# Dense products of two batches leave their bank by ScalarE instead of VectorE's fused blend, and all queues get new orders

## The chip, the cores and the metric

The kernel runs on one core of one Trainium2 chip. The time is the device time of one execution in microseconds (us), the median of several runs. A profiled execution shows every instruction. The engines are TensorE (PE: matrix products, and PEld for its weight loads), VectorE (DVE), ScalarE (ACT), GpSimd (POOL) and SyncE (SP), whose queue (SPq) issues all transfers here. Matrix products are written into banks of PSUM; everything else lies in SBUF, and transfers go between SBUF and the chip's memory (HBM).

## The reference

Four stages run over x of 4 batches x 512 tokens x 512 features, each with a layer norm and a residual:

```python
x = x + attn_a(layernorm(x))   # gelu(x @ (w1.T-w2.T product * sparse_mask) + b2)
x = x + ffn(layernorm(x))
x = x + attn_b(layernorm(x))   # one head of 128: softmax(q k^T) v, times Wo
x = x + ffn(layernorm(x))

def ffn(x):                    # weight 512x512, 64 centroids
    dots = softmax(x @ centroids.T / TEMPERATURE)
    hits = dots > THRESHOLD
    query_sel = any(hits, axis=1)              # per token
    cluster_sel = any(hits, axis=0)            # over ALL tokens
    row_sel = cluster_sel[assignments]         # per output feature
    dense = x @ weight.T + bias
    return where(query_sel[:, None] & row_sel[None, :], dense, 0)
```

The row selection of a feed-forward stage needs the softmax of all 2,048 tokens, so no output of stage 4 can be finished before the clusters of its last batch are known.

## The kernel before

The tokens are cut into 16 tiles of 128 (batch b, tile t; n = 4b + t). Every fp32 operand is split into a high and a low part, so one 128x128 by 128x512 product is three matmuls. Five tables, PE_ORDER, ACT_ORDER, DVE_ORDER, POOL_ORDER and SP_ORDER, list by hand every step of every queue; each engine walks its table from front to back, and a step waits on the semaphores of what it needs. An engine whose next step is not ready waits, and all behind it wait too. PE writes into four banks for products (m_bank) and four for transposes (t_bank). Each kind takes them in rotation in the order of PE_ORDER, so a new tile waits until the tile that stood in the same bank four tiles earlier was taken out (`freed_by`).

Steps of stage 4, for batch b and tile t:

- T.x4.b.t: PE transposes x after stage 3; hi.x4 (ACT) and lo.x4 (DVE) split the result.
- cl4.b.h: products with the centroids (a batch at once, or a half); lgev (ACT, L649) copies them out, tc (PE) transposes them, logit, lmax (DVE, L881 to L888), cexp (ACT, L671) and prob (DVE, L895 to L905) do the softmax. prob writes `qsel` (query_sel of the batch's tokens), `rq` = rstd * qsel, and the running maximum `best`.
- After the last batch, best1 (DVE, L910), bestT (PE, L1070), csel (DVE, L915 and L917) and mask (PE, L1086) turn `best` into a bank that holds row_sel for every token. The rest of `out` hangs on it.
- dn4.b.t.c...: the dense products of a tile, in chunks of the 512 inputs (c02 is chunks 0 and 2). The layer norm's mean lies in the weights, its rstd is applied afterwards.
- qb.b.t (ACT, L719): y_tok = qsel * bias. xb.b.t (POOL, L546): y_tok += x_tok. blend4.b.t (DVE, L925): y_tok = bank * rq + y_tok. That frees the bank.
- out.b.t (DVE, L949) copies y_tok over x_tok where the mask bank says so, and store.b.t (SP) writes the tile to HBM.
- The last tile, 3.3, goes in two halves of 256 columns: dn4h, blend4h (L936), outh (L942), storeh.

Stage 2 has the same steps with a 2. There the dense products already leave through ACT: ev2 (L664, y_tok = rstd * bank), bias2 (POOL, L526), and blend2 or x2 on DVE (L829, L842: y_tok * qsel + x_tok, both operands in SBUF). In stage 3, norm.3, bo.b.t (POOL, L540) and x3.b.t (DVE, L872) appear in the rows below. In stage 1, attn.0.0, attn.0.1 and attn.0.2 are four matmuls each (L1019): w1_hi*w2_hi, w1_hi*w2_lo, w1_lo*w2_hi; T.x1 transposes the normed x of batch 0 (norm.1.0.t on ACT), and w2lo (L738) and w1lo (L743) are the low parts of the weights, made on DVE between the statistics of x (stats, L768 and L769).

Of the kernel before, what the change touches and what calls it, by code (L numbers as in the profile page):

```python
# [26 lines left out]

SQUARED = {2, 3, 4}
# [1157 lines left out]
```

## Time and profile before

| | |
|---|---|
| median of 3 runs | 279.13 us (278.44 to 280.58) |
| the profiled execution | 278.25 us, of which the core's span is 276.5 us |
| PE busy | 268.4 us (97% of the span) |
| DVE, ACT, POOL busy | 196.7, 176.8, 158.8 us (71%, 64%, 57%) |
| TensorE's granted clock over the span | 0.997 of 2.4 GHz |
| HBM read, written | 13.76 MB, 4.19 MB |

Times within the span count from its start. A line number is a line of the kernel before. A row of instructions that are alike is merged ("x6"); its duration is then from the first start to the last end. "[0.59 <-PE ...]" behind a row is the time in which the engine sat idle before it and what ended the wait. PE's matmuls overlap in the pipeline: one is shown 0.39 us long, while the next starts 0.23 us later.

### The profile page before, as it was taken

The page shows a single profiled execution, that of the slowest core. Times are in us where ns is not written, and L with a number is a line of the kernel's source. Part 1 is how long each engine was busy: PE and PEld are TensorE (multiplying, and loading weights), DVE is VectorE, ACT ScalarE, POOL GpSimd, SP SyncE. Part 2 cuts the span into 40 slices and gives each one's busy share as a digit, 9 for nine tenths or more (in the row PEclk, how much of TensorE's full clock was granted, in tenths as well). Part 3 has the DMA queues.
Part 4 walks back from the last instruction along what each step waited for, and adds up shares of the span by engine and source line. Part 5 has one row for each costly group of instructions (what it writes and reads, how often), then busy time and mean ns, then how long its engine had stood idle before and what let it go on. Part 6 is the DMA issues. An engine that isn't in the chain of part 4 may idle for free.

```text
span 276.5 us, 4419 instructions
## 1 busy us (share of the span) xinstructions
PE 268.4 (97%) x1392; PEld 224.2 (81%) x1392; DVE 196.7 (71%) x410; ACT 176.8 (64%) x358; POOL 158.8 (57%) x192
## 2 busy tenths in 40 slices
PE   7899999999999999999999999999999999999894
PEld 7787888888888888789988888888888888877673
DVE  3888988505926867775399796788259466867996
ACT  4855886465476785449899887777645576675400
POOL 4693988265495481289897994970730537113910
PEclk9999999999999999999999999999999999999998
DMA  6999064800000000000000000000000000000087
GB/s 230 356 370 344 12 207 177 303 0 0 2 0 0 2 0 2 2 0 0 2 0 0 4 1 0 2 0 0 2 2 0 0 2 1 0 2 0 13 306 288
DMA packets 10246, 18.23 MB, mean 66 GB/s; under 512 B 1200, under 2 KB 1968, under 8 KB 10224
## 3 DMA queue, kind: packets, MB, share of 16 engines
q1 hardware_dynamic: 10224, 17.96, 18.5%
q8 instruction: 11, 0.18, 0.3%
q14 instruction: 11, 0.09, 0.1%
HBM read 13.76 MB, written 4.19 MB: 65 GB/s over the span
## 4 chain that ended last, share of the span: by engine, by line
PE 88%; issue 4%; POOL 2%; DVE 2%; DMA 2%; ACT 1%; SPq 1%; DVEq 0%; POOLq 0%; ACTq 0%
PE m_bank L966 70%; PE t_bank L1059 11%; PE m_bank L1139 5%; DMA x_tok<-in_L_attn_a_x 2%; POOL y_tok L546 1%; PE t_bank L1065 1%; PE m_bank L1019 1%; DVE y_tok L925 1%; DVE x_tok L949 0%; ACT odd_hi L613 0%; POOL rstd L458 0%; SPq L384 0%; DVE y_tok L936 0%; SPq L387 0%; PE m_bank L1086 0%
## 5 line engine op out<-in xcount | busy, mean ns | idle before, releaser
L966 PE MATMUL m_bank<-ffn_hi,even_hi 128*128 128x512 f32 x96 | 39.0, 406 | 0.2 <-DVE y_tok L925 0.2
L966 PE MATMUL m_bank<-ffn_lo,even_hi 128*128 128x512 f32 x96 | 37.7, 392 | 0.0
L966 PE MATMUL m_bank<-ffn_hi,even_lo 128*128 128x512 f32 x96 | 37.4, 390 | 0.0
L546 POOL TENSOR_TENSOR y_tok<-y_tok,x_tok 128x512 f32<-128x512 f32 x16 | 20.4, 1296 | 25.4 <-ACT y_tok L719 25.4
L570 ACT ACTIVATE ones_and_squares<-x_tok,mv 128x512 bf16<-128x512 f32 x44 | 31.5, 717 | 4.1 <-DVE x_tok L872 3.7
L526 POOL TENSOR_TENSOR y_tok<-y_tok,bias_f 128x512 f32<-128x512 f32 x16 | 20.8, 1314 | 16.2 <-ACT y_tok L664 16.2
L454 POOL TENSOR_SCALAR ve<-mv 128x1 f32<-128x1 f32 (+1 forms) x20 | 5.3, 264 | 36.1 <-ACT ones_and_squares L570 35.0
L458 POOL TENSOR_TENSOR rstd<-ve,half 128x1 f32<-128x1 f32 (+1 forms) x31 | 23.9, 771 | 2.6
L775 DVE TENSOR_TENSOR even_lo<-t_bank,even_hi 128x512 fp32r<-128x512 f32 x24 | 16.2, 683 | 12.7 <-ACT even_hi L613 12.5
L775 DVE TENSOR_TENSOR odd_lo<-t_bank,odd_hi 128x512 fp32r<-128x512 f32 x28 | 18.8, 685 | 6.2 <-ACT odd_hi L613 6.0
L966 PE MATMUL m_bank<-odd_hi,wqkv_hi 128*128 128x512 f32 (+1 forms) x60 | 21.5, 358 | 0.0
L966 PEld LDWEIGHTS m_bank<-ffn_lo,even_hi 128*128 128x128 f32 x96 | 18.0, 188 | 3.9
L540 POOL TENSOR_TENSOR x_tok<-x_tok,bo 128x512 f32<-128x512 f32 x16 | 21.0, 1331 | 0.0
L966 PEld LDWEIGHTS m_bank<-ffn_hi,even_hi 128*128 128x128 f32 x96 | 18.1, 188 | 3.6 <-DVE y_tok L925 0.6
L966 PE MATMUL m_bank<-odd_lo,wqkv_hi 128*128 128x512 f32 (+1 forms) x60 | 20.9, 348 | 0.0
L966 PE MATMUL m_bank<-odd_hi,wqkv_lo 128*128 128x512 f32 (+1 forms) x60 | 20.8, 347 | 0.0
L966 PEld LDWEIGHTS m_bank<-ffn_hi,even_lo 128*128 128x128 f32 x96 | 18.1, 189 | 3.1
L966 PE MATMUL m_bank<-attn_hi,odd_hi 128*128 128x512 f32 x48 | 19.5, 405 | 0.0
L581 ACT ACTIVATE xn_odd<-x_tok,ve,rstd 128x512 f32<-128x512 f32 x20 | 16.1, 811 | 4.8 <-POOL ve L461 4.8
L966 PE MATMUL m_bank<-attn_lo,odd_hi 128*128 128x512 f32 x48 | 18.8, 391 | 0.0
L966 PE MATMUL m_bank<-attn_hi,odd_lo 128*128 128x512 f32 x48 | 18.7, 390 | 0.0
L613 ACT ACTIVATE even_hi<-t_bank 128x512 fp32r<-128x512 f32 x24 | 13.8, 595 | 6.8 <-PE t_bank L1059 6.8
(186 smaller groups left out, 775.2 us busy)
## 6 DMA issues: line engine op xcount, KB each, us to landing
out<-x_tok SPq DMA_DIRECT2D x15, 256.0 KB, 2.3
x_tok<-in_L_attn_a_x SPq DMA_DIRECT2D x3, 1024.0 KB, 8.2
xn_odd<-in_L_attn_a_xt SPq DMA_DIRECT2D x2, 1024.0 KB, 6.5
x_tok<-in_L_attn_a_x SPq DMA_DIRECT2D x4, 256.0 KB, 4.2
y_tok<-in_L_attn_a_w SPq DMA_DIRECT2D x4, 256.0 KB, 5.1
w_raw<-in_L_attn_a_w SPq DMA_DIRECT2D x4, 256.0 KB, 5.3
xt_other<-in_L_ffn_weight SPq DMA_DIRECT2D x4, 256.0 KB, 6.8
y_tok<-in_L_attn_a_sparse_mask SPq DMA_DIRECT2D x4, 256.0 KB, 7.3
```

Of the source, the lines that this page charges most:

```text
L454: link(pool.tensor_scalar(ve[:, i:i + k], mv[:, i:i + k, 1], 1.0 / D ** 3, EPS, ALU.mult, ALU.add))
L458: ins = pool.tensor_tensor(rstd[:, i:i + k], ve[:, i:i + k], half[:, 0:k], ALU.pow)
L526: pool.tensor_tensor(y_tok[:, n, :], y_tok[:, n, :], bias_f[:, :], ALU.add).then_inc(done[kind], 1)
L540: pool.tensor_tensor(x_tok[:, n, :], x_tok[:, n, :], bo[:, :], ALU.add).then_inc(done[kind], 1)
L546: pool.tensor_tensor(y_tok[:, n, :], y_tok[:, n, :], x_tok[:, n, :], ALU.add).then_inc(done[kind], 1)
L570: act.activation(squares, x_tok[:, n, :], ACT.Square, bias=sum_of(*key), scale=-float(D), accum_out=mv[:, i, 1:2]).then_inc(done[kind], 1)
L581: act.activation(xn_odd[:, t, :], x_tok[:, n, :], ACT.Identity, bias=nbias[:, i:i + 1], scale=rstd[:, i:i + 1]).then_inc(done[kind], 1)
L613: act.activation(split_of(what, b, t)[0], bank_view(what, bank_of("T", *key)), ACT.Copy).then_inc(done[kind], 1)
L775: dve.tensor_tensor(lo, bank_view(what, bank_of("T", *key)), f32(hi), ALU.subtract).then_inc(done[kind], 1)
L966: ins = pe.matmul(bank, a, w, start=(first and n == 0), stop=(last and n == count - 1))
L1059: ins = pe.transpose(bank[:, c * r:(c + 1) * r], blk, ident[0:r, 0:r])
L1139: ins = pe.matmul(bank[:, tokens], cen_hl[:, c, :], a[:, c, tokens], start=(c + h == 0), stop=(c == KC - 1 and h == 1))
```

## The change

For the tiles of batches 2 and 3 except 3.3 (seven tiles), the three steps qb, xb and blend4 are replaced. ev4 (ACT) reads the bank and writes y_tok = rstd * bank; bias4 (POOL) adds the bias; blend4 (DVE) computes y_tok * qsel + x_tok with both operands in SBUF. The bank is free after ev4. Each engine has as many steps of these kinds as before.

```diff
+EVICTED = {2, 3}
...
+                elif kind == "bias4":
+                    b, t = key
+                    n = b * TPB + t
+                    pool.wait_ge(*done_at("ev4", (b, t)))
+                    pool.tensor_tensor(y_tok[:, n, :], y_tok[:, n, :], bias_f[:, :], ALU.add).then_inc(done[kind], 1)
...
+                elif kind == "ev4":
+                    b, t = key
+                    n = b * TPB + t
+                    i = 3 * NT + n
+                    act.wait_ge(*done_at("dn4", key))
+                    act.wait_ge(*done_at("rstd", (4, b)))
+                    act.wait_ge(*done_at("x2", (b, t)))
+                    act.activation(y_tok[:, n, :], bank_of("dn4", b, t)[:, :], ACT.Identity,
+                                   scale=rstd[:, i:i + 1]).then_inc(done[kind], 1)
...
+                elif kind == "blend4" and key[0] in EVICTED:
+                    b, t = key
+                    n = b * TPB + t
+                    dve.wait_ge(*done_at("bias4", key))
+                    dve.wait_ge(*done_at("prob", (4, b)))
+                    dve.scalar_tensor_tensor(out=y_tok[:, n, :], in0=y_tok[:, n, :], scalar=qsel[:, 1, n:n + 1],
+                                             in1=x_tok[:, n, :], op0=ALU.mult, op1=ALU.add).then_inc(done[kind], 1)
...
+                if kind == "dn4" and key[0] in EVICTED:
+                    return done_at("ev4", key)
...
```

All five tables are new from their first entry to their last: the tiles of every stage come in another order (PE begins its transposes with tile 0.1 instead of 0.0, for instance), and so do the loads and stores. The number of products, transposes, splits and transfers is the same. SP's last four entries were store.3.1, store.2.2 and the two halves of 3.3; now they are store.3.2, the two halves of 3.3, and store.2.1.

One line of PE_ORDER near its end, before and now:

```diff
-dn4.2.3.c3 dn4.3.0.c31 dn4.3.2.c2 bestT.4 dn4.3.1.c0 dn4.2.2.c1 mask.4 dn4.3.1.c1 dn4.3.2.c03 dn4.2.2.c3
...
+dn4.3.0.c2 bestT.4 dn4.2.2.c0 mask.4 dn4.3.1.c2 dn4.2.2.c3 dn4.3.1.c30 dn4.2.1.c3 dn4.2.2.c21 dn4.3.2.c1
```

PE's first steps. The rows are the two groups of four L1019 matmuls behind the first transpose, before the change; even_lo is w1's low part (w1lo), w2t_lo is w2's (w2lo):

```order
L1019 MATMUL m_bank<-w2t_hi,even_hi 128x512 [waits w1hi_done,w2hi_done,consts]
L1059 MATMUL t_bank<-ident,xn_odd 128x128 [waits norm_done]
L1019 MATMUL m_bank<-w2t_lo,even_hi 128x512 [waits w2lo_done]
L1019 MATMUL m_bank<-w2t_hi,even_lo 128x512 [waits w1lo_done]
L1059 MATMUL t_bank<-ident,xn_odd 128x128 [waits norm_done]
```

The same place of PE in the changed kernel:

```order
L1045 MATMUL m_bank<-w2t_hi,even_hi 128x512 [waits w1hi_done,w2hi_done,consts]
L1085 MATMUL t_bank<-ident,xn_odd 128x128 [waits norm_done]
L1045 MATMUL m_bank<-w2t_hi,even_lo 128x512 [waits w1lo_done]
L1045 MATMUL m_bank<-w2t_lo,even_hi 128x512 [waits w2lo_done]
L1085 MATMUL t_bank<-ident,xn_odd 128x128 [waits norm_done]
```

The group that needs w1's low part now comes ahead of the one that needs w2's.

DVE's queue from best1 of stage 4 to the last output tile, before the change (L925 is blend4, L949 and L942 are out and outh, L936 is blend4h):

```order
L910 TENSOR_REDUCE best<-best 128x64 [waits prob_done]
L925 SCALAR_TENSOR_TENSOR y_tok<-m_bank,rq,y_tok 128x512 [waits prob_done,xb_done,dn4_done]
L915 TENSOR_REDUCE csel<-t_bank 64x1 [waits bestT_done]
L917 TENSOR_SCALAR csel<-csel 64x128 [waits chain]
L925 SCALAR_TENSOR_TENSOR y_tok<-m_bank,rq,y_tok 128x512 [waits prob_done,xb_done,dn4_done]
L949 COPY_PREDICATED x_tok<-m_bank,y_tok 128x512 [waits blend4_done,mask_done] x6
...
L936 SCALAR_TENSOR_TENSOR y_tok<-m_bank,rq,y_tok 128x256 [waits prob_done,xb_done,dn4h_done]
L942 COPY_PREDICATED x_tok<-m_bank,y_tok 128x256 [waits blend4h_done,mask_done] x2
```

The same place of DVE in the changed kernel (L941 is the blend4 of the seven tiles, L973 and L966 are out and outh, L960 is blend4h):

```order
L927 TENSOR_REDUCE best<-best 128x64 [waits prob_done]
L941 SCALAR_TENSOR_TENSOR y_tok<-y_tok,qsel,x_tok 128x512 [waits prob_done,bias4_done]
L932 TENSOR_REDUCE csel<-t_bank 64x1 [waits bestT_done]
L934 TENSOR_SCALAR csel<-csel 64x128 [waits chain]
L941 SCALAR_TENSOR_TENSOR y_tok<-y_tok,qsel,x_tok 128x512 [waits prob_done,bias4_done]
L973 COPY_PREDICATED x_tok<-m_bank,y_tok 128x512 [waits blend4_done,mask_done] x4
L941 SCALAR_TENSOR_TENSOR y_tok<-y_tok,qsel,x_tok 128x512 [waits prob_done,bias4_done]
L973 COPY_PREDICATED x_tok<-m_bank,y_tok 128x512 [waits blend4_done,mask_done] x5
L941 SCALAR_TENSOR_TENSOR y_tok<-y_tok,qsel,x_tok 128x512 [waits prob_done,bias4_done] x2
...
L941 SCALAR_TENSOR_TENSOR y_tok<-y_tok,qsel,x_tok 128x512 [waits prob_done,bias4_done]
L966 COPY_PREDICATED x_tok<-m_bank,y_tok 128x256 [waits blend4h_done,mask_done]
L973 COPY_PREDICATED x_tok<-m_bank,y_tok 128x512 [waits blend4_done,mask_done]
```

The blends read no bank any more, one blend that stood ahead of best1 has moved behind it, five blends of full tiles now stand behind the first out where four stood, and the last entry is a full tile.

ACT's last rows in the changed kernel (L657 is lgev, L679 cexp, L689 ev4, L736 qb); before, the L689 rows were eight L719 rows (qb), two ahead of the last cexp and six behind it:

```order
L657 ACTIVATE lg<-m_bank 128x512 [waits tc_done,cl4_done]
L689 ACTIVATE y_tok<-m_bank,rstd 128x512 [waits x2_done,rstd_done,dn4_done]
L679 ACTIVATE ce<-cl,ncmx,rstd 128x64 [waits lmax_done]
L679 ACTIVATE ce<-cl,ncmx,rstd 128x64 x3
L689 ACTIVATE y_tok<-m_bank,rstd 128x512 [waits x2_done,rstd_done,dn4_done] x2
L736 ACTIVATE y_tok<-bias_f,qsel 128x512 [waits x2_done,prob_done]
L689 ACTIVATE y_tok<-m_bank,rstd 128x512 [waits x2_done,rstd_done,dn4_done] x4
```

ACT's last steps now wait for PE's tiles, where they waited for prob only.

## Rows read from the trace of the kernel before

**Rows 1.** Busy time by stretch: stretch, us, each engine's busy us, clock, DMA share, GB/s.

```profile
220.00:240.00 20.00, 20.00 (x107) 16.80 (x106) 14.19 (x32) 12.23 (x27) 9.73 (x9) 1.00 0.01 1
...
250.00:260.00 10.00, 8.68 (x38) 6.46 (x37) 7.83 (x15) 6.17 (x12) 6.31 (x6) 1.00 0.00 1
```

**Rows 2.** Chain of work that ended last: start us, us, what.

```profile
7.84 0.67 DVE w2t_lo L738
...
70.96 0.44 PE t_bank L1065 x4
71.40 5.49 PE m_bank L966 x24
```

**Rows 3.** Timeline of PE: start, us, line, what, idle before it.

```profile
7.25 0.60 PE L1059 MATMUL t_bank<-ident,xn_odd 128*128 128x128 f32 x4
8.55 1.21 PE L1019 MATMUL m_bank<-w2t_lo,even_hi 128*128 128x512 f32 x4 [0.70 <-DVE w2t_lo L738]
...
10.53 0.60 PE L1059 MATMUL t_bank<-ident,xn_odd 128*128 128x128 f32 x4
...
241.31 0.39 PE L1139 MATMUL m_bank<-even_hi,cen_hl 128*128 128x512 f32 x1
...
249.02 0.63 PE L1065 MATMUL t_bank<-ident,lg 128*128 128x128 f32 x4
...
256.14 0.50 PE L966 MATMUL m_bank<-ffn_hi,odd_hi 128*128 128x512 f32 x1 [0.33 <-DVE y_tok L925]
...
259.60 0.50 PE L1086 MATMUL m_bank<-onehot,csel 128*128 128x512 f32 x1 [0.98 <-DVE y_tok L925]
```

**Rows 4.** Timeline of ACT at the start.

```profile
7.65 0.63 ACT L558 ACTIVATE even_hi<-y_tok 128x512 fp32r<-128x512 f32 x1 [0.68 <-DMA y_tok<-in_L_attn_a_w]
```

**Rows 5.** Timeline of DVE, from the last softmax to the mask.

```profile
253.26 1.30 DVE L897 TENSOR_SCALAR qsel<-crec 128x4 f32<-128x4 f32 x1
...
255.01 0.42 DVE L905 TENSOR_TENSOR best<-best,cl 128x256 f32<-128x256 f32 x1
...
257.58 1.30 DVE L917 TENSOR_SCALAR csel<-csel 64x128 fp32r<-64x128 f32 x1
258.81 0.73 DVE L925 SCALAR_TENSOR_TENSOR y_tok<-m_bank,rq,y_tok 128x512 f32<-128x512 f32 x1
```

**Rows 6.** Timeline of POOL in the same stretch.

```profile
253.26 1.28 POOL L546 TENSOR_TENSOR y_tok<-y_tok,x_tok 128x512 f32<-128x512 f32 x1 [0.95 <-ACT y_tok L719]
256.26 7.54 POOL L546 TENSOR_TENSOR y_tok<-y_tok,x_tok 128x512 f32<-128x512 f32 x6 [1.72 <-ACT y_tok L719]
```

**Rows 7.** Single lines: duration ns min/median/max, first and last start us.

```profile
L897 DVE TENSOR_SCALAR qsel<-crec x8: 169/170/1300, 86.7 to 253.3; 128x4 f32<-128x4 f32 x8
...
L842 DVE SCALAR_TENSOR_TENSOR x_tok<-y_tok,qsel,x_tok x12: 735/752/1436, 122.7 to 174.0; 128x512 f32<-128x512 f32 x12
...
L526 POOL TENSOR_TENSOR y_tok<-y_tok,bias_f x16: 1287/1312/1349, 66.2 to 162.7; 128x512 f32<-128x512 f32 x16
...
L664 ACT ACTIVATE y_tok<-m_bank,rstd x16: 671/687/696, 53.6 to 129.6; 128x512 f32<-128x512 f32 x16
```

**Rows 8.** Timeline of DVE, then of POOL, where stage 2's blend met a POOL operation.

```profile
155.14 1.44 DVE L842 SCALAR_TENSOR_TENSOR x_tok<-y_tok,qsel,x_tok 128x512 f32<-128x512 f32 x1
...
154.74 3.02 POOL L540 TENSOR_TENSOR x_tok<-x_tok,bo 128x512 f32<-128x512 f32 x2
```

**Rows 9.** Timeline of DVE behind the mask: its first and its last row.

```profile
260.13 3.91 DVE L949 COPY_PREDICATED x_tok<-m_bank,y_tok 128x512 f32<-128x512 int32 x6 [0.59 <-PE m_bank L1086]
...
273.42 0.76 DVE L942 COPY_PREDICATED x_tok<-m_bank,y_tok 128x256 f32<-128x256 int32 x2
```

**Rows 10.** Busy time of DVE behind the mask: stretch, us, busy us, clock, DMA.

```profile
260.13:274.20 14.07, 13.77 (x23) 1.00 0.71 266
```

**Rows 11.** Transfers by line: KB each, median us from issue to landing.

```profile
out<-x_tok SPq DMA_DIRECT2D x15, 256.0 KB, 2.3
...
out<-x_tok SPq DMA_DIRECT2D x2, 128.0 KB, 1.8
```

More of the change, by code:

```diff
@@ L80 @@
[L80 to L84 removed]
+w1hi.0 w2hi.0 norm.1.0.1 w2hi.1 w1hi.1 hi.x1.0.1 norm.1.0.2 w2hi.3 w1hi.3 w2hi.2 w1hi.2 norm.1.0.0 hi.x1.0.2
@@ L85 @@
+ev4.2.3 cexp.4.3 ev4.2.0 ev4.3.0 qb.3.3 ev4.3.1 ev4.2.2 ev4.2.1 ev4.3.2
 """
 DVE_ORDER = """
[L88 to L91 removed]
@@ L97 @@
-logit.2.2 lo.x2.3.0 lmax.2.2 lo.x2.3.2 prob.2.2 logit.2.3 lmax.2.3 blend2.2 blend2.1 prob.2.3 best1.2 csel.2
-x2.0.3 x2.0.0 stats.3.0.3 stats.3.0.0 x2.0.2 x2.0.1 stats.3.0.2 stats.3.0.1 x2.1.3 lo.x3.0.3 lo.x3.0.2 lo.x3.0.0
-lo.x3.0.1 x2.1.2 x2.1.1 x2.1.0 qkdve.q.0 qkdve.k.0 max.0.0 lo.x3.1.3 lo.x3.1.1 lo.x3.1.2 lo.x3.1.0 max.0.1
-max.0.2 max.0.3 lo.p.0.0 x2.2.0 x2.2.3 lo.v.0.0 x2.2.1 x2.2.2 lo.p.0.1 qkdve.k.1 qkdve.q.1 lo.p.0.2 lo.p.0.3
-max.1.3 max.1.2 x2.3.0 lo.x3.2.0 lo.x3.2.3 max.1.0 olo.0 max.1.1 lo.x3.2.1 lo.x3.2.2 rden.0 rden.1 x3.0.0
@@ L107 @@
-rden.3 blend4.1.3 lo.p.3.0 lo.p.3.1 x3.2.1 blend4.1.0 blend4.1.2 lo.x4.2.3 olo.3 lo.x4.2.2 lo.x4.2.0 x3.3.2
-x3.3.0 blend4.1.1 lo.x4.2.1 x3.3.3 lo.x4.3.2 x3.3.1 lo.x4.3.0 lo.x4.3.1 logit.4.2 lmax.4.2 lo.x4.3.3 prob.4.2
-logit.4.3 lmax.4.3 prob.4.3 blend4.2.3 best1.4 blend4.2.1 csel.4 blend4.3.0 out.0.1 out.2.3 out.0.0 out.1.1
-out.1.0 out.0.2 blend4.3.2 out.1.3 out.3.2 out.3.0 out.0.3 out.2.1 blend4.3.1 out.1.2 blend4.2.0 blend4.2.2
-out.2.0 out.3.1 blend4h.3.3.0 out.2.2 blend4h.3.3.1 outh.3.3.0 outh.3.3.1
+stats.1.0.1 w1lo.0 stats.1.0.2 w2lo.0 stats.1.0.0 w2lo.1 stats.1.0.3 w1lo.1 w2lo.3 w1lo.3 w2lo.2 w1lo.2 cstat
@@ new lines @@
+stats.1.2.0 lo.x2.1.1 logit.2.0 stats.1.3.2 scaled.2.3 lmax.2.0 x1.2.3 scaled.2.0 scaled.2.2 x1.2.2 x1.2.0
+stats.1.3.3 prob.2.0 scaled.3.3 logit.2.1 x1.3.3 scaled.2.1 lmax.2.1 blend2.1 x1.2.1 scaled.3.0 blend2.0
+scaled.3.2 blend2.3 lo.x2.2.3 lo.x2.2.2 x1.3.0 lo.x2.3.0 lo.x2.2.1 lo.x2.3.3 x1.3.2 lo.x2.2.0 scaled.3.1
+lo.x2.3.2 x1.3.1 blend2.2 prob.2.1 logit.2.2 lmax.2.2 lo.x2.3.1 prob.2.2 logit.2.3 lmax.2.3 prob.2.3 best1.2
+csel.2 x2.0.0 x2.0.3 stats.3.0.0 stats.3.0.3 x2.0.2 stats.3.0.2 x2.0.1 stats.3.0.1 x2.1.2 lo.x3.0.2 lo.x3.0.0
@@ L112 @@
+lo.x4.3.2 prob.4.2 logit.4.3 lmax.4.3 prob.4.3 best1.4 blend4.2.3 csel.4 blend4.2.0 out.0.2 out.2.0 out.1.3
+out.1.1 blend4.3.0 out.2.3 out.0.3 out.1.0 out.0.1 out.0.0 blend4.3.1 blend4.2.2 out.3.0 out.2.2 out.3.1 out.1.2
+blend4h.3.3.0 blend4.3.2 blend4h.3.3.1 out.3.2 outh.3.3.0 blend4.2.1 outh.3.3.1 out.2.1
 """
 POOL_ORDER = """
-rstd.1.0.0 rstd.1.0.1 rstd.1.0.2 rstd.1.0.3 fsum.1 fsum.2 fsum.3 asum.1 cmean asum.2 asum.3 alo.0 xlo.1.0 alo.2
-alo.3 xlo.1.2 alo.1 xlo.1.3 xlo.1.1 rstd.1.1 flo.0 latehi.2 flo.1 flo.2 rstd.2.0 flo.3 xlo.2.0 latehi.0 xlo.2.2
@@ L130 @@
[L130 to L133 removed]
+load.x0.1 load.w1.0 load.w2.0 load.x0.2 load.x0.0 load.w2.1 load.w1.1 load.x0.3 load.w2.3 load.w1.3 load.w2.2
@@ L134 @@
+load.w1.2 load.ffn.1 load.ffn.0 load.cen load.ffn.2 load.ffn.3 load.sparse.0 load.sparse.1 load.sparse.2
+load.sparse.3 load.xt.1 load.b2 load.small load.x.1 load.bias load.x.3 load.late load.x.2 load.xt.3 load.xt.2
+store.1.1 store.2.0 store.0.2 store.1.0 store.1.3 store.0.3 store.0.0 store.2.3 store.3.0 store.0.1 store.1.2
+store.3.1 store.2.2 store.3.2 storeh.3.3.0 storeh.3.3.1 store.2.1
 """
```

147 lines of the change are left out of this document (72 added, 75 removed).

## The prediction

> **What bounds the kernel now.** PE is busy for 97% of the span, but that share is an average, so I read the busy times by stretch first. Between 220 and 240 us PE is busy for all of 20 us, and every other engine has a quarter to a half of its time free [rows 1]. A PE step costs 5.49 / 24 = 0.229 us per product of 512 columns and 0.44 us per four transposes [rows 2]. Counted with these, the new PE table holds the same 261.6 us of work as the old one, so the change can only move the places where PE doesn't run, and what follows its last product.
>
> There are two such places. At the start PE has its first transpose done at about 7.7 us and waits until 8.55 for w2's low part [rows 2, 3]. At the end, from 250 to 260 us, it is busy for 8.68 of 10 us [rows 1]: it waits for a bank before 256.14, and before the mask at 259.60 for csel and then for a blend that frees the mask's bank [rows 3]. Behind the mask the bound is another engine. DVE runs 23 instructions in 14.07 us and is busy for 13.77 of them [rows 10], from the first out at 260.13 to the last at 273.42 + 0.76 = 274.18 [rows 9]. Then comes only the last store; the span ends at 276.5. So the end is set by two things: when the mask is ready, and how much DVE still has to do behind it.
>
> **The change, part by part.** Durations come from the profiled execution of 278.25 us (span 276.5). The median of the runs is 279.13, 0.9 more; I add that at the end.
>
> *Seven evictions.* ACT: one reading of a bank costs 0.69 us, about the same as the qb that it replaces [rows 7]. POOL: bias4 for xb, 1.31 us each, as before [rows 7]. DVE: the blend from two SBUF operands has a median of 0.75 us in stage 2 [rows 7], and the blend from the bank takes 0.73 [rows 5]. By durations alone this part costs nothing. The bank comes free after ACT instead of after the softmax: that takes away the wait before 256.14 and the blend in front of the mask.
>
> *Start.* The group that needs w1's low part now stands first, and w2's low part is made one statistics step earlier, so the 0.86 us wait at 8.55 goes. But the next transpose needs norm.1.0.2, and ACT has a weight split beginning at 7.65 with the weight's arrival [rows 4], then another split, a hi and the norm: 0.6 + 0.6 + 0.6 + 0.8 puts it at about 10.3. It stood at 10.53 [rows 3]. I take -0.2 of a possible -0.86.
>
> *Middle.* Ahead of tc, PE waits for ACT's copy of the cl bank. From 241.31 to tc.4.3 the old table holds 7.1 us of work, which would end at 248.4, and tc began at 249.02 [rows 3]: 0.6 us went in such waits. In stages 2 and 4 one chunk of products (0.69 us) stood between the last cl and its tc; two stand there now. Elsewhere I counted the PE work between a product and the step that needs it; the shortest distances are about those of before (1.1 us where a blend of 0.75 us frees the bank). I take the products from 241.31 on 0.25 us earlier with the start in, with a range of -0.9 to +1.5 for small new waits in the 230 us between.
>
> *To the mask.* tc.4.3 stood at 249.02 [rows 3]. In the new table 8.5 us of work stand ahead of it; from 241.05, with 0.15 for what is left of the waits, it begins at 249.7, and the last logit starts at 250.4 where it was 249.75. Then lmax, an ev4 that lies under it on ACT, cexp and the sums. In the kernel before, the tiny qsel instruction took 1.30 us against a median of 0.17 [rows 7], because POOL's addition ran from 253.26 to 254.54 [rows 5, 6]; the same happened at csel, 1.30 us from 257.58, until POOL's next addition ended at 258.8. In the new order ev4.2.0 follows cexp directly, so bias4.2.0 starts just as qsel does: held again, for the same 1.1 us. The running maximum ends at 256.2 (before: 255.01 + 0.42 = 255.43). best1 0.6, then the blend of 2.3, which the new order puts in front of csel, 0.7; csel's first half 0.3. bias4.3.0 has started at 257.45, so csel's second half is held until 258.7 and ends at 258.9. The mask needs nothing else now: 258.95 against 259.60, **-0.65** (this includes the -0.25).
>
> *Behind the mask.* The blend of 2.0 lies in the mask's own 0.5 us and ends at 259.6, so the first out starts there and not at 260.13: **-0.5**. Five full blends instead of four follow: **+0.7**. The last store is a full tile, landing 2.3 us after its issue, where it was a half tile with 1.8 [rows 11]: **+0.5**. The sum is +0.7, if no blend meets a POOL addition.
>
> *Meeting POOL.* This is the term that the old tail did not have: its blends have one SBUF operand, and the one at 258.81 took 0.73 us while POOL was adding [rows 5, 6]. The new ones are of stage 2's kind. There one started at 155.14, 0.4 us behind the start of a POOL addition, and took 1.44 us, and the pair of additions took 3.02 us instead of 2.6 [rows 8]: they took turns. In the new tail POOL has six additions of 1.3 us from 257 us on, and DVE five blends. If each blend waits as long as it can, 2.0 waits 1.25 for xb.3.3, 3.0 waits 0.85, 3.1 waits 0.2, 2.2 waits 1.3: together +3.6. The low end is 0, since the median of stage 2's 12 blends is 0.75 us [rows 7]. I take **+1.1**, the measured hold of one small instruction, nearest to one full meeting. The sum: +0.7 + 1.1 = +1.8, a span of 278.3 us and 279.13 + 1.8 = **280.9 us**.
>
> The Trainium skill, SBUF — State Buffer, section "SBUF: two separate sides", says that DVE and GpSimd share one pair of ports, and that a DVE operation with two SBUF inputs and a GpSimd operation that reads SBUF exclude each other for the whole instruction. By that rule, the trace agrees: 1.44 for 0.75 us at 155.14. The page speaks against the change, and taken at its full length at every meeting it gives the +3.6.
>
> **The rivals.**
>
> *Slower: the blends queue behind POOL.* The place is DVE's first blend behind csel. If POOL's xb.3.3 starts before it, the first out slips from 259.6 to 260.8, and the later blends then fall onto bias4.3.1 and bias4.3.2 as priced above. It decides as soon as more than two full POOL additions (2.6 us) are waited out. Time: 279.13 + 0.7 + 3.6 = 283.4. For it: DVE has no idle time there (0.3 us in 14) to absorb anything. Against it: POOL must wait for ACT, and ACT for PE, so from 263 us on its additions come one per 2 us and leave gaps. Two SBUF operands, and the wait taken in full, are also what the page's rule gives.
>
> *No meeting.* The blends fall into POOL's gaps: +0.7, 279.8 us. For it: the median of stage 2's blends [rows 7]. Against it: there the blend followed on its own tile's POOL step; here POOL's next one is already waiting for it.
>
> *Faster: the holds vanish.* If POOL's additions miss qsel and csel (2 x 1.1 us) the mask comes when PE reaches it, at about 257.2. The first out is then 1.9 earlier than in my sum: -1.2, 277.9 us. With the whole start gain of 0.86 the mask would follow, to 277.2. For it: the additions now start when an ev4 ends, not when prob ends. Against it: both ev4s end within 0.3 us of the DVE instructions.
>
> *A new wait in the middle.* All orders are new, and one late tile that stalls PE by 2 us or more puts the time at 283 or above. Against it: the spare distances named above.
>
> **How the numbers follow.** About 1% is what a measurement of this kernel can tell from no change; that is 276.3 and 281.9. Forecast (280.2 to 281.9) 0.40; no meeting 0.24; holds vanish 0.09, of which 0.03 go below 276.3; blends queue 0.21; wait in the middle 0.06. Slower: 0.21 + 0.06, and 0.04 of the forecast's edge, 0.31. Faster 0.03. Same 0.66. The range leaves out the lower half of the holds case and the worst of the last two: 278.5 to 283.4. The side within 1% holds most of the chance; its own range is 278.5 to 281.9.
>
> **What would show it.** PE's second group at about 7.7 us and no wait at 8.55; the next transpose near 10.3. PE without idle time until about 256.5. qsel and csel of stage 4's last batch at 1.3 us. The mask at 259.0, the first out at 259.6, or at 260.8 if the slower rival holds. Blends of the new line with durations over 1.0 us: one or two for the forecast, four for the slower rival, none for the other. The last store 2.3 us before the end. I would be wrong if the mask moved by more than 1 us, or if PE had idle time between 15 and 240 us of more than 1 us.

## The result, and the profile after

| | before | after |
|---|---|---|
| median of the runs, us | 278.80 (278.44 to 280.58) | 282.34 (281.89 to 285.01) |
| ratio to before, 95% interval | | 1.0149 (1.0120 to 1.0177) |
| profiled execution, us (span) | 278.25 (276.5) | 282.29 (280.5) |
| PE idle, 0 to 20 us | 2.52 | 3.34 |
| PE idle, 100 to 120 us | 0.09 | 2.42 |
| PE idle, 140 to 160 us | 0 | 0.42 |
| cl4.2 begins | 241.31 | 245.21 |
| mask.4 begins | 259.60 | 262.77 |
| first out | 260.13 | 263.28 |
| DVE's last instruction ends | 274.18 | 278.07 |

The change makes the kernel slower by 1.3% by the medians and by 1.5% by the ratio. The forecast of 280.9 us was 1.4 us too low, and the loss isn't where it was placed: cl4.2 already comes 3.9 us later, with the same steps of PE ahead of it in both tables, and from there to the end of the span the two kernels need almost the same (35.19 and 35.29 us). So I start with the busy times by stretch of the kernel after (columns as in [rows 1]), to see where PE stood still.

```profile
0.00:20.00 20.00, 16.66 (x83) 13.80 (x83) 12.20 (x24) 12.30 (x20) 13.17 (x30) 1.00 0.81 269
100.00:120.00 20.00, 17.58 (x90) 14.22 (x89) 14.62 (x30) 11.56 (x26) 11.52 (x11) 1.00 0.00 1
120.00:140.00 20.00, 20.00 (x132) 18.15 (x131) 13.08 (x27) 13.78 (x25) 16.12 (x28) 1.00 0.01 2
140.00:160.00 20.00, 19.58 (x109) 16.25 (x108) 16.55 (x35) 17.67 (x38) 15.59 (x22) 1.00 0.00 0
250.00:260.00 10.00, 10.00 (x55) 8.60 (x54) 6.32 (x18) 5.19 (x13) 3.80 (x4) 1.00 0.00 0
```

The same view of the kernel before, 100 to 120 us:

```profile
100.00:120.00 20.00, 19.91 (x104) 16.30 (x102) 15.47 (x38) 10.95 (x27) 7.90 (x10) 1.00 0.01 2
```

PE lost 2.42 us in stage 2's last softmax and selection, where before it lost 0.09; POOL is busy there for 11.5 us instead of 7.9. Between 250 and 260 us, where PE lost 1.3 us before [rows 1], it now loses nothing. PE's timeline after, at the start, in stages 2, 3 and 4 (the rows of stage 4 answer to [rows 3]):

```profile
11.22 0.66 PE L1085 MATMUL t_bank<-ident,xn_odd 128*128 128x128 f32 x4 [1.18 <-ACT xn_odd L589]
117.21 0.27 PE L1096 MATMUL t_bank<-ident,best 128*64 128x128 f32 x1 [1.60 <-DVE best L927]
119.09 0.47 PE L1112 MATMUL m_bank<-onehot,csel 128*128 128x512 f32 x1 [0.82 <-issue]
142.22 0.63 PE L1085 MATMUL t_bank<-ident,xn_odd 128*128 128x128 f32 x4 [0.42 <-DVE odd_lo L792]
245.21 0.40 PE L1165 MATMUL m_bank<-even_hi,cen_hl 128*128 128x512 f32 x1
260.89 0.27 PE L1096 MATMUL t_bank<-ident,best 128*64 128x128 f32 x1 [0.38 <-DVE best L927]
262.77 0.47 PE L1112 MATMUL m_bank<-onehot,csel 128*128 128x512 f32 x1 [0.82 <-issue]
```

In stage 2 PE waits 1.60 us for the running maximum and 0.82 us before the mask. DVE's and POOL's timelines of that place, after:

```profile
109.43 1.40 DVE L922 TENSOR_TENSOR best<-best,cl 128x256 f32<-128x256 f32 x1
114.37 1.27 DVE L914 TENSOR_SCALAR qsel<-crec 128x4 f32<-128x4 f32 x1
117.83 1.16 DVE L934 TENSOR_SCALAR csel<-csel 64x128 fp32r<-64x128 f32 x1
109.00 2.99 POOL L529 TENSOR_TENSOR y_tok<-y_tok,bias_f 128x512 f32<-128x512 f32 x2
114.32 1.30 POOL L529 TENSOR_TENSOR y_tok<-y_tok,bias_f 128x512 f32<-128x512 f32 x1 [2.34 <-ACT y_tok L672]
116.41 2.50 POOL L529 TENSOR_TENSOR y_tok<-y_tok,bias_f 128x512 f32<-128x512 f32 x2 [0.80 <-ACT y_tok L672]
```

and before:

```profile
108.88 0.42 DVE L905 TENSOR_TENSOR best<-best,cl 128x256 f32<-128x256 f32 x1
113.21 0.17 DVE L897 TENSOR_SCALAR qsel<-crec 128x4 f32<-128x4 f32 x1
115.59 0.22 DVE L917 TENSOR_SCALAR csel<-csel 64x128 fp32r<-64x128 f32 x1
115.76 2.56 POOL L526 TENSOR_TENSOR y_tok<-y_tok,bias_f 128x512 f32<-128x512 f32 x2 [9.35 <-ACT y_tok L664]
```

This is the hold that the prediction described at the end of the kernel, now in stage 2. Each of the three small DVE instructions ends within 0.1 us of the end of a POOL addition: 1.40 for 0.42, 1.27 for 0.17, 1.16 for 0.22 us, 3.0 us together. (The first, the running maximum at 109.43, belongs to batch 2; the other two to the last batch.) Before, POOL had been idle for 9.35 us and took up its additions only 0.17 us after csel began. What changed is where the bias additions of stage 2 stand in POOL's table (and their evictions in ACT's):

```
before: ... rstd.2.2 latelo.2 bias2.0.1 rstd.2.3 bias2.2.0 bias2.2.2 rstd.3.0.3 ...
after:  ... rstd.2.3 latelo.3 latelo.0 bias2.1.2 bias2.3.0 bias2.2.3 bias2.3.3 bias2.2.0 rstd.3.0.0 ...
```

Five stand between rstd.2.3 and the first rstd of stage 3 now, two did before.

### The profile page after: what moved, and what is told of

It is laid out like the page before. It is cut to its first block, busy times and chain, and to the rows that moved or that the text cites. A ratio compares the mean times of both kernels' runs of the same rounds, so it can differ in the third digit from the quotient of the medians.

```text
span 280.5 us, 4419 instructions
## 1 busy us (share of the span) xinstructions
PE 267.6 (95%) x1392; PEld 224.2 (80%) x1392; DVE 200.2 (71%) x410; ACT 177.1 (63%) x358; POOL 162.0 (58%) x192
## 4 chain that ended last, share of the span: by engine, by line
PE 84%; DVE 6%; ACT 3%; DMA 2%; issue 2%; SPq 1%; DVEq 0%; ACTq 0%
PE m_bank L990 67%; PE t_bank L1085 11%; PE m_bank L1165 4%; DMA y_tok<-in_L_attn_a_w 2%; ACT ce L679 2%; DVE qsel L914 1%; PE t_bank L1091 1%; DVE best L922 1%; DVE cl L898 1%; DVE csum L912 1%; ACT odd_hi L621 1%; DVE cmx L903 0%; ACT L679 0%; SPq L387 0%; SPq L390 0%
## 5 line engine op out<-in xcount | busy, mean ns | idle before, releaser
L554 POOL TENSOR_TENSOR y_tok<-y_tok,x_tok 128x512 f32<-128x512 f32 x9 | 12.2, 1372 | 22.7 <-ACT y_tok L736 22.7
L457 POOL TENSOR_SCALAR ve<-mv 128x1 f32<-128x1 f32 (+1 forms) x20 | 6.1, 304 | 32.1 <-ACT ones_and_squares L578 31.2
L792 DVE TENSOR_TENSOR even_lo<-t_bank,even_hi 128x512 fp32r<-128x512 f32 x24 | 16.0, 682 | 11.5 <-ACT even_hi L621 11.4
L621 ACT ACTIVATE odd_hi<-t_bank 128x512 fp32r<-128x512 f32 x28 | 16.0, 593 | 4.6 <-PE t_bank L1085 2.4
```

The costliest lines, as they stand in the source:

```text
L457: link(pool.tensor_scalar(ve[:, i:i + k], mv[:, i:i + k, 1], 1.0 / D ** 3, EPS, ALU.mult, ALU.add))
L554: pool.tensor_tensor(y_tok[:, n, :], y_tok[:, n, :], x_tok[:, n, :], ALU.add).then_inc(done[kind], 1)
L621: act.activation(split_of(what, b, t)[0], bank_view(what, bank_of("T", *key)), ACT.Copy).then_inc(done[kind], 1)
L792: dve.tensor_tensor(lo, bank_view(what, bank_of("T", *key)), f32(hi), ALU.subtract).then_inc(done[kind], 1)
```

## The experiments

Times below are medians. The changed kernel's 282.34 us comes from the runs of the result. The variants were timed in other sets of runs, each with the kernel before beside it on the same chip, and its median went from 278.60 to 279.06 us between the sets. So where two variants lie close together, their ratios to the kernel before are the safer comparison. "PE idle" is worked out from the busy times by stretch.

**1. Take the holds of stage 2 away.** The kernel after, and on POOL:

```diff
+ if key == (1, 2):
+     pool.wait_ge(*done_at("csel", (2,)))
- bias2.1.2 bias2.3.0 bias2.2.3 bias2.3.3 bias2.2.0 rstd.3.0.0 ... rstd.3.0.1 masked.1.0 masked.1.3
+ bias2.1.2 bias2.3.0 bias2.2.3 rstd.3.0.0 ... rstd.3.0.1 masked.1.0 bias2.3.3 masked.1.3 bias2.2.0
```

> The changed kernel, but POOL's bias additions of stage 2 from bias2.1.2 on wait until csel.2 is done, and bias2.3.3 and bias2.2.0 stand behind the rstd sums and masked copies of stage 3. Same work. Theory 1 (POOL's additions, moved under stage 2's last softmax, hold its small DVE instructions): qsel falls from 1.27 to about 0.17 us, best from 1.40 to about 0.42, csel from 1.16 to about 0.22; the mask of stage 2, now at 119.09, comes about 2.4 us earlier (about 116.7), and the whole kernel takes about 280.0 us, 2.4 less than the changed kernel. Rival (the chain is late for its PE order or its place in ACT's queue, and POOL only fills time that is lost anyway): the mask moves by less than 0.5 us and the total by less than 0.5.

282.30 us, where the kernel after has 282.34 (ratios 1.0119, 1.0059 to 1.0179, and 1.0149): the rival's time, by a way that the rival did not have. The mask did come 3.5 us earlier, 0.9 of it from an earlier start (PE's first y1 product began at 10.85 instead of 11.73 us), and PE then stood still twice in stage 3. PE's timeline of this kernel:

```profile
115.63 0.47 PE L1114 MATMUL m_bank<-onehot,csel 128*128 128x512 f32 x1
124.42 1.50 PE L1087 MATMUL t_bank<-ident,xn_odd 128*128 128x128 f32 x12 [0.81 <-ACT xn_odd L591]
133.67 0.35 PE L992 MATMUL m_bank<-odd_hi,wqkv_hi 128*128 128x256 f32 x1 [1.68 <-DVE odd_lo L794]
```

The first wait is my edit's fault: three additions (3.81 us) now stand between csel and the first rstd of stage 3, which needs POOL. I took the second for a delay of the changed kernel itself. Its DVE order has x2.1.3 and x2.1.0, which wait for POOL's masked copies, ahead of lo.x3.0.1, which stage 3's first products need. DVE does that one at 132.85 us here, and at 132.95 in the kernel after, where PE comes late enough for it. DVE's timeline of this kernel, then POOL's:

```profile
130.47 1.77 DVE L861 SCALAR_TENSOR_TENSOR x_tok<-y_tok,qsel,x_tok 128x512 f32<-128x512 f32 x1 [1.75 <-POOL y_tok L543]
132.85 0.68 DVE L794 TENSOR_TENSOR odd_lo<-t_bank,odd_hi 128x512 fp32r<-128x512 f32 x1
127.89 1.29 POOL L531 TENSOR_TENSOR y_tok<-y_tok,bias_f 128x512 f32<-128x512 f32 x1
129.14 1.30 POOL L543 TENSOR_TENSOR y_tok<-y_tok,rows 128x512 f32<-128x512 f32 x1
130.40 1.29 POOL L531 TENSOR_TENSOR y_tok<-y_tok,bias_f 128x512 f32<-128x512 f32 x1
```

POOL's rows say otherwise: this wait is my edit's making too. bias2.3.3, which I had put ahead of masked.1.3, runs at 127.89 and makes that copy 1.3 us later, and DVE's x2.1.3 waits for it. bias2.2.0, behind it at 130.40, holds x2.1.3 itself, 1.77 us for 0.75. Without these 2.3 us lo.x3.0.1 would end at about 131.2 instead of 133.5, where PE was ready at 131.99 (133.67 less the wait of 1.68): an estimate, but by it PE would have waited for nothing there. That the two kernels do lo.x3.0.1 at almost the same time is a coincidence. So the null result does not acquit the holds of stage 2. I read it as a second delay hidden behind the first, and experiments 2 and 3 were built on that reading.

**2. The order of lo.x3.0.1 alone.** The kernel after, and on DVE:

```diff
- lo.x3.0.3 x2.1.3 x2.1.0 lo.x3.0.1 x2.1.1
+ lo.x3.0.3 lo.x3.0.1 x2.1.3 x2.1.0 x2.1.1
```

> The same kernel as e9_lo_first again, since TensorE's granted clock was 0.984 in its profiled execution (the changed kernel's was 0.996) and its times lay between 281.40 and 284.58 us. Theory (the DVE order alone gives nothing while the mask is late): 282.0 to 282.7 us, within 0.4 of the changed kernel. Rival: 281 us or below.

282.80 us, ratio 1.0145 (1.0118 to 1.0171), with the same idle time as the kernel after (2.43 us in 100 to 120, 0.43 in 140 to 160). No gain; the median lies 0.1 us above the range that I had given. A first set of runs of the same kernel had a median of 283.33, 1.0 above the changed kernel where I had expected less than 0.4, and its profiled execution a granted TensorE clock of 0.92 between 120 and 140 us. Its rows show where: from 120 to 123 us the granted clock was 0.50, the lower level of 1.2 GHz, behind waits of PE of 1.60 and 0.82 us (up to 117.87 and 119.75). The first kernel of experiment 7 shows the same, 0.50 from 119 to 121 us behind waits of 1.59 and 0.84 us. Three other profiled executions with these waits (the kernel after, this one, experiment 5) kept 1.00. So in some executions the waits of stage 2 cost more than their own length.

**3. The holds away, with room, and the DVE edit of 2.** The DVE edit of 2, bias2.1.2 waiting for lmax.2.3 and bias2.3.0 for csel.2, and bias2.2.0 and bias2.3.3 put just ahead of their own masked copies:

```diff
- bias2.1.2 bias2.3.0 bias2.2.3 bias2.3.3 bias2.2.0 rstd.3.0.0
+ bias2.1.2 bias2.3.0 bias2.2.3 rstd.3.0.0
- rstd.3.1.0 masked.2.0    (and: rstd.3.2.2 masked.3.3)
+ rstd.3.1.0 bias2.2.0 masked.2.0    (and: rstd.3.2.2 bias2.3.3 masked.3.3)
```

> The changed kernel with both delays between stage 2's softmax and stage 3's first products taken away. POOL: bias2.1.2 waits for lmax.2.3 (it then lies under ACT's exponentials), bias2.3.0 and what follows wait for csel.2, and bias2.2.0 and bias2.3.3 move behind the rstd steps of stage 3, just ahead of their own masked copies. DVE: lo.x3.0.1, which stage 3's first products need, goes ahead of x2.1.3 and x2.1.0, which wait for POOL. Same work. Theory (two delays stand one behind the other: POOL's holds move stage 2's mask by 3.1 us, and lo.x3.0.1 would be ready only at about 133 us anyway; taking away the first alone gave nothing, since PE then waited 0.8 us at 124 and 1.7 us at 134): with both gone PE is busy from 20 to 140 us, cl4.2 comes 2 to 3 us earlier, and the total is about 280.0 us (2.3 less than the changed kernel). Rival (POOL's total work in stage 3 is the limit, so the idle time only moves on to the next batch, 141 to 160 us): total within 0.7 us of the changed kernel.

280.51 us (280.21 to 281.07), 1.8 less than the kernel after, ratio to the kernel before 1.0066 (1.0041 to 1.0092). Busy times by stretch:

```profile
100.00:120.00 20.00, 20.00 (x102) 16.38 (x101) 14.33 (x36) 11.86 (x26) 9.33 (x11) 1.00 0.01 2
120.00:140.00 20.00, 19.57 (x135) 17.81 (x135) 11.14 (x24) 15.25 (x28) 16.42 (x27) 1.00 0.00 1
140.00:160.00 20.00, 19.28 (x102) 15.57 (x101) 16.74 (x37) 17.36 (x37) 17.80 (x24) 1.00 0.00 0
```

Put beside each other, PE's idle time from 100 to 160 us and the time agree:

| kernel | PE idle, 100 to 160 us | median, us |
|---|---|---|
| before | 0.09 | 278.80 |
| after | 2.84 | 282.34 |
| 1: additions moved behind csel | 2.92 | 282.30 |
| 2: lo.x3.0.1 earlier | 2.86 | 282.80 |
| 3: lo.x3.0.1 earlier, and additions placed with room | 1.15 | 280.51 |

This kernel differs from that of experiment 2 by the POOL edit alone. The ratios to the kernel before are 1.0066 (1.0041 to 1.0092) and 1.0145 (1.0118 to 1.0171), so taking the additions out from under the softmax is worth 2.3 us, or 1.8 against the changed kernel, for 1.7 us less idle time. The DVE edit by itself gave nothing. Whether it adds anything on top of the POOL edit wasn't run. POOL's masked copies and DVE's lo.x3.0.1 in this kernel speak against it:

```profile
126.26 2.56 POOL L544 TENSOR_TENSOR y_tok<-y_tok,rows 128x512 f32<-128x512 f32 x2
129.43 0.69 DVE L795 TENSOR_TENSOR odd_lo<-t_bank,odd_hi 128x512 fp32r<-128x512 f32 x1 [1.07 <-ACT odd_hi L624]
```

Stage 3's rows are 2.73 us earlier here than in the kernel after. In the old DVE order lo.x3.0.1 would start at about 130.2 instead of 132.95 and end at 130.9, and PE needs it at about 131.5 (an estimate from these rows). The remaining 1.15 us are two waits of T steps for norms, 0.43 and 0.72 us. The rival of this experiment, POOL's work in stage 3, may have a share in them; that was not separated.

**4. Put the cause into the kernel before.** Two additions of stage 2 go under its last softmax:

```diff
+ if key == (2, 3):
+     pool.wait_ge(*done_at("cexp", (2, 3)))
- rstd.2.3 bias2.2.0 bias2.2.2
+ rstd.2.3 bias2.2.3 bias2.3.3 bias2.2.0 bias2.2.2
```

> The kernel before with the suspected cause put in: two of stage 2's bias additions that POOL made later go under the last softmax, bias2.2.3 as soon as cexp.2.3 is done (about 112.5 us) and bias2.3.3 behind it (about 115.1 us, when its eviction is done). Same work, POOL has it done earlier. Theory (POOL's additions hold the small DVE instructions, and PE stands at the mask): qsel (113.21, 0.17 us) or its neighbour takes 0.5 us more, csel (115.59, 0.22 us) 0.8 more, PE waits 1.0 to 1.5 us at bestT.2 and mask.2, the total rises by 0.8 to 1.6 us. Rival (such holds are absorbed, since the stages overlap): total within 0.4 us of the kernel before.

279.53 us against 279.06, ratio 1.0021 (1.0006 to 1.0036): +0.5 us, below what I expected. The interval runs from 0.2 to 1.0 us, so the loss is clear of zero, but the time by itself doesn't exclude the rival, which allowed 0.4. The instructions do show the mechanism. DVE and POOL in this kernel:

```profile
112.75 0.42 DVE L896 TENSOR_REDUCE csum<-ce 128x4 f32<-128x256 f32 x1 [0.17 <-ACT ce L672]
113.21 0.18 DVE L897 RECIPROCAL crec<-csum 128x4 f32<-128x4 f32 x1
113.42 0.69 DVE L898 TENSOR_SCALAR qsel<-crec 128x4 f32<-128x4 f32 x1
116.31 0.46 DVE L918 TENSOR_SCALAR csel<-csel 64x128 fp32r<-64x128 f32 x1
112.80 1.29 POOL L527 TENSOR_TENSOR y_tok<-y_tok,bias_f 128x512 f32<-128x512 f32 x1 [6.18 <-ACT ce L672]
```

qsel was held for 0.52 us, as expected, but csel for 0.24 only, since the first hold had moved it nearly clear of the next addition. PE's idle time from 100 to 120 us rose from 0.09 to 0.62, by the amount of the loss. The mechanism shows when it is put in and when it is taken out; the size of a hold depends on tenths of a microsecond of alignment.

**5. The holds of stage 4 in the kernel after.**

```diff
+ if key == (2, 0):
+     pool.wait_ge(*done_at("csel", (4,)))      # in front of bias4
- csel.4 blend4.2.0 out.0.2 out.2.0 out.1.3 out.1.1 blend4.3.0
+ csel.4 out.0.2 out.1.3 out.1.1 blend4.2.0 out.2.0 blend4.3.0
```

> The changed kernel, but in stage 4 bias4.2.0 and everything behind it on POOL wait until csel.4 is done, and on DVE three outs that need no late blend go ahead of the blend of 2.0. Same work. Theory 1 (holds by POOL at qsel and csel are on the path to stage 4's mask): qsel 0.17 and csel 0.22 instead of 1.27 and 1.04; the mask 1.3 us earlier than now measured from cl4.2 (PE's work then sets it), the total about 1.2 us less than the changed kernel, near 281.1. Rival 1 (DVE's work behind the mask sets the end, and the additions that were put off now fall beside its blends): the mask comes earlier but the total stays within 0.4. Rival 2 (the holds are not POOL's): qsel and csel stay above 1 us and nothing moves.

282.70 us, ratio 1.0134 (1.0083 to 1.0184), no gain: rival 1. qsel took 0.17 and csel 0.22 us, and the first out came 2.3 us earlier, at 261.01, of which 0.8 had come from the start. But DVE's last instruction ended at 277.40 instead of 278.07. DVE needed 16.39 us from the first out to its end, where the kernel after needs 14.79. The blend of 2.0 now stands behind the first out, 0.7 us of this, and blends met POOL's additions:

```profile
268.43 2.45 DVE L942 SCALAR_TENSOR_TENSOR y_tok<-y_tok,qsel,x_tok 128x512 f32<-128x512 f32 x2
268.60 1.72 POOL L535 TENSOR_TENSOR y_tok<-y_tok,bias_f 128x512 f32<-128x512 f32 x1 [0.74 <-ACT y_tok L690]
```

The pair took 2.45 us where it took 1.80 after and takes 1.41 undisturbed. The addition that it met waited for ACT and is not one of those that were put off. Counted from cl4.2 (244.41 us here) DVE ends after 32.99 us, where it was 32.86 after: the earlier mask was used up behind it.

**6. The same in the kernel before,** whose blends read a bank:

```diff
- lgev.4.3 qb.2.0 qb.2.1 cexp.4.3 qb.2.3 qb.3.0
+ lgev.4.3 qb.2.1 qb.2.3 cexp.4.3 qb.3.0 qb.2.0
+ if key == (2, 0):
+     pool.wait_ge(*done_at("csel", (4,)))      # in front of xb
```

> The kernel before, with two edits in stage 4: ACT's qb.2.1 and qb.2.3 go ahead of cexp.4.3 so that the blends have what they need, and POOL's xb.2.0 and all behind it wait until csel.4 is done. Same work. Theory 1 (in the kernel before too, POOL's additions hold qsel by 1.1 and csel by 1.1 us on the path to the mask): qsel 0.17 and csel 0.22 us, the mask 1.5 to 2.2 us earlier than 259.60, the total 1.2 to 2 us below the kernel before, near 277. Rival (DVE's work behind the mask grows by what the additions put off, or the qb steps delay the exponential): total within 0.5 us of the kernel before.

277.24 us, 0.9943 (0.9918 to 0.9969) of the kernel before: 1.6 us faster by the ratio, and 5.1 us below the changed kernel. It is the best version found. Counted from cl4.2 (242.18) the mask comes 16.69 us later, where it was 18.29, so 1.6 us less; in the profiled execution a start that was 0.9 us later hides part of it. Its DVE rows (those of before are in [rows 5, 9]):

```profile
254.77 0.17 DVE L898 TENSOR_SCALAR qsel<-crec 128x4 f32<-128x4 f32 x1
257.93 0.22 DVE L918 TENSOR_SCALAR csel<-csel 64x128 fp32r<-64x128 f32 x1
272.68 0.76 DVE L943 COPY_PREDICATED x_tok<-m_bank,y_tok 128x256 f32<-128x256 int32 x2
```

POOL's additions run beside these blends and outs too, and cost them nothing: from the first out at 259.40 to the end at 273.44 DVE needs 14.04 us, as before (14.05).

**7. The evictions by themselves.** First the other way round, the kernel after without them: qb and xb in the places of ev4 and bias4, and also other orders of DVE's last twenty steps (the blend of 2.3 ahead of best1, that of 2.0 ahead of csel) and of the last stores. The line that switches the evictions off:

```diff
- EVICTED = {2, 3}
+ EVICTED = set()
```

> The changed kernel's new orders of all queues, but without the seven evictions: the dense products of batches 2 and 3 leave their bank by DVE's fused blend again (qb on ACT and xb on POOL in the places of ev4 and bias4; DVE's last twenty steps and the last stores are put in an order that this allows). Same work. Theory 1 (the loss comes from the new orders, ahead of 241 us): the total stays at 281.5 us or above, cl4.2 at about 245 us. Rival (the evictions themselves cost it): the total falls back to 280 or below. For the tail alone: the evictions are worth between -1 and +1 us, so this one should be 281.5 to 283.5.

287.11 us. The middle is as in the kernel after (17.57 of 20 us busy in 100 to 120), so the orders alone carry that loss. By the profile the other 5.2 us, against the kernel after, lie in two places. 1.3 us come before cl4.2 (246.55 instead of 245.21), with the granted clock at 0.96 and 0.95 in the two stretches from 100 to 140 us (see experiment 2). 3.9 us lie between cl4.2 and the end of the span, 39.15 instead of 35.29 us. There PE waits for banks that DVE's blends free, and the granted clock is 0.83 from 260 to 270 us, behind a wait of 2.37 us that ended at 262.17. Waits of PE in this kernel (total, times, longest):

```profile
PE m_bank L989 <- DVE y_tok L948: 4.0, 2, 2.4
PE m_bank L1111 <- DVE y_tok L948: 1.4, 1, 1.4
```

Whether the new PE order or the place of the blends on DVE makes these waits was not separated.

Then the evictions alone in the kernel before:

> The kernel before with its own orders, and the evictions alone: the seven dense tiles of batches 2 and 3 of stage 4 leave their bank by ScalarE, get their bias on POOL and are blended by DVE from SBUF. In the last 20 steps of DVE and the last stores the tile of 2.0 changes place with 2.2 and the halves, as far as the new waits need it. Same work. Theory (evictions only move a blend from ahead of the mask to behind it, and DVE is the limit there): mask and first out 0.4 to 0.7 us earlier, the last out 0 to 1.0 later, total between -0.3 and +1.2 us of the kernel before, best guess +0.4. Rival 1 (the evictions are a gain, which the new orders threw away): total 1 us or more below. Rival 2 (they cost the time themselves, by meeting POOL's additions): total 2 us or more above.

284.45 us, ratio 1.0207 (1.0172 to 1.0242), 5.9 us slower: the number of rival 2, and partly its way. Four blends ran beside POOL's additions and took 1.73, 1.25, 1.77 and 1.44 us where they take 0.74, 3.2 us more together. The rest is my placing: ev4.2.1 stood in ACT's table ahead of cexp.4.3 and made the exponentials wait for a product, and DVE's blend of 2.3 stood ahead of best1 and waited for POOL; PE waited 2.6 us for best. That says what a badly placed eviction costs, not what one is worth. So once more, with room (ACT: cexp.4.3 ev4.2.1 ev4.2.3 ev4.3.0; POOL's first bias4 waits for csel.4; DVE: best1.4 csel.4, four outs, and then the seven blends between outs):

> The kernel before with its own orders, and the evictions alone, placed with more room than in e7_evict_only: ACT does the first eviction behind cexp.4.3, POOL's first bias addition of stage 4 waits until csel.4 is done, and on DVE all seven blends stand behind csel, with at least two outs between one and the next where the tiles allow it. Same work. Theory (an eviction lets the mask go before its blends, but each blend then lies behind the mask, where DVE is the limit): qsel 0.17 and csel 0.22 us, mask near 257.8 and first out near 258.3 instead of 260.13, DVE's work behind it 14.07 + 3 x 0.7 = 16.2 us and 0.5 to 2 us of meetings; the last out ends at 275.0 to 276.5 instead of 274.2, the total 0.8 to 2.3 us above the kernel before. Rival (well placed, the evictions are worth their while): total at or below the kernel before.

280.20 us, ratio 1.0055 (1.0035 to 1.0075): 1.5 us slower by the ratio. The first out comes 1.9 us earlier and the last ends 1.5 us later.

```profile
256.93 0.22 DVE L933 TENSOR_SCALAR csel<-csel 64x128 fp32r<-64x128 f32 x1
258.22 2.65 DVE L972 COPY_PREDICATED x_tok<-m_bank,y_tok 128x512 f32<-128x512 int32 x4 [1.08 <-PE m_bank L1111]
263.58 1.34 DVE L940 SCALAR_TENSOR_TENSOR y_tok<-y_tok,qsel,x_tok 128x512 f32<-128x512 f32 x1
270.15 1.62 DVE L940 SCALAR_TENSOR_TENSOR y_tok<-y_tok,qsel,x_tok 128x512 f32<-128x512 f32 x2
274.96 0.76 DVE L965 COPY_PREDICATED x_tok<-m_bank,y_tok 128x256 f32<-128x256 int32 x2
```

An eviction lets the mask go before its blends, but puts each blend behind the mask, where DVE is the limit: DVE needs 17.5 us from the first out instead of 14.05, of which three more blends are 2.2 and meetings with POOL and waits the rest.

**8. The start.** The kernel of experiment 6, with PE's attn.0.2 ahead of attn.0.1:

> The kernel before with the two stage-4 edits of e4_before_free, and at the start PE's product group attn.0.2 (which needs w1's low part) ahead of attn.0.1 (which needs w2's low part, ready 0.7 to 0.9 us too late). Same work. Theory: the wait for w2's low part goes (0.7 us in the last profile), the later transposes follow 0.4 to 0.7 us earlier, and the total is 0.3 to 0.8 us below e4_before_free, near 276.7. Rival (the transpose behind waits for its norm instead, since the loads set the start): within 0.2 us of e4_before_free, 277.2.

277.54 us against 277.24, ratios 0.9956 (0.9938 to 0.9973) and 0.9943: the rival's time, but not for the rival's reason. No transpose waited for its norm. The product group behind waited instead, for the next low part of w2:

```profile
11.10 0.49 PE L966 MATMUL m_bank<-w2t_hi,even_hi 128*128 128x512 f32 x1 [0.59 <-DVE w2t_lo L738]
```

Over the profiled executions with the changed tables (seven) PE is busy in the first 20 us for 16.66 to 18.20 us, mean 17.27, and with the old ones (five) for 16.82 to 17.79, mean 17.31. That first y1 product begins at 10.85 to 12.32 us (mean 11.44) with the changed tables and at 10.83 to 12.01 (mean 11.26) with the old ones. The start differs from execution to execution by more than the orders differ.

## Why the prediction was right or wrong

- **What bounds the kernel now:** right for the end, and the wrong place to stop. PE without idle time between 20 and 240 us was taken as safe, where it meant that every chain there just about made it.
- **Evictions by duration:** right. ACT's take 0.69, POOL's additions 1.3 and DVE's new blends 0.73 to 0.75 us.
- **Start, -0.2:** in the profiled execution +0.8: 0.5 from a wait of 1.18 us at 11.22 in place of the old one at 8.55, which is 0.70 us in its row, not 0.86, and 0.3 from a longer wait before the first product group (1.18 for 0.84). The steps of ACT ahead of that transpose were the right ones, but its weight split could begin only when the weight arrived, at 8.62 us here and not at 7.65, after 1.46 us of idle time. Over the executions above the two orders are equal. The order gains nothing, and the 0.8 of the 4.0 us between the two profiled executions can be such spread.
- **Middle, -0.05: this is the step that failed.** I counted PE work between a product and the step that needs it, and took that for the spare distance. What the chain between them would take was left as it was, although POOL's table had changed under it. The hold that I priced at qsel and csel of stage 4 was not looked for at the same instructions of stage 2, 140 us earlier. The holds took 3.0 us of DVE's time there, PE's idle time from 100 to 120 us rose from 0.09 to 2.42 us, it went when the additions stood elsewhere (experiments 1 and 3), and experiment 3 against experiment 2 gives 2.3 us for it. A further 0.4 us stand in a wait at 142 us. I had given "a new wait in the middle" 0.06; it was the case that came true, and so did both signs that I had named for being wrong: the mask moved by 3.2 us, and PE had 2.8 us of idle time in the middle.
- **To the mask:** right in its parts. Counted from cl4.2 it is 17.56 us away instead of 18.29, 0.7 less, where my steps gave 0.4 less. qsel and csel were held as forecast (1.27 and 1.04 us) and PE waited for no blend before the mask. DVE's rows after, and POOL's addition from which the meetings below are read:

```profile
257.98 1.27 DVE L914 TENSOR_SCALAR qsel<-crec 128x4 f32<-128x4 f32 x1
263.28 2.61 DVE L973 COPY_PREDICATED x_tok<-m_bank,y_tok 128x512 f32<-128x512 int32 x4
262.55 1.94 POOL L554 TENSOR_TENSOR y_tok<-y_tok,x_tok 128x512 f32<-128x512 f32 x1
```

- **First out:** 18.07 us behind cl4.2 instead of 18.82, 0.75 less; forecast 0.3 less.
- **Fifth blend, +0.7:** right. From the first out to the end DVE takes 14.79 instead of 14.05 us, +0.74. These include the meeting below; the 0.3 us that DVE was idle there before are gone.
- **Last store, +0.5:** mis-sized. From DVE's last end to the end of the span it is 2.4 us after and 2.3 before, +0.1. The medians over all stores [rows 11] did not tell of the last one.
- **Meetings with POOL, +1.1:** mis-sized, +0.4. Only one pair was stretched:

```profile
269.55 1.80 DVE L941 SCALAR_TENSOR_TENSOR y_tok<-y_tok,qsel,x_tok 128x512 f32<-128x512 f32 x2
277.36 0.71 DVE L973 COPY_PREDICATED x_tok<-m_bank,y_tok 128x512 f32<-128x512 int32 x1
```

  Elsewhere POOL was the one to wait: its addition from 262.55 us took 1.94 us for 1.3, while the blend of 2.0 (from 262.60) took its usual 0.73.

From cl4.2 to the end my steps gave +2.05 us and the profile +0.1; up to cl4.2 they gave -0.25 and the profile +3.9. That the forecast came within 1.4 us is luck: the two errors have opposite signs. Of the 3.9 us, 0.8 lie in the start and 2.75 in the waits of stages 2 and 3; 0.3 us I can't place. Of the 3.5 us between the medians the holds of stage 2 are shown for 1.8 (experiment 3 against the changed kernel; 2.3 against experiment 2). The rest of stage 3's waits and the tail were not separated further.

## What to carry to other kernels

When all orders are new, follow every chain that has to meet a busy engine, and look at what the other queues now run under it, not only at the work that covers it. A cost found at one instruction is looked for at every place where that instruction stands. An edit that takes a delay away without gain acquits that delay only if the wait has not come back through the edit's own placing: look at what now stands behind the work that was moved, and move work from one side of a gate to the other only if the engine there has time for it. To price one cause, compare two kernels that differ in one table alone.
